# Two MLPs whose first pieces are moved into the stages ahead of them, in a four-layer cross-attention kernel

## The chip, the cores and the metric

The kernel runs on one core of a Trainium2 chip, written directly for the five engines with hand-placed semaphores. TensorE (PE) multiplies and transposes, VectorE (DVE) and ScalarE (ACT) work elementwise, GpSimd (POOL) takes smaller elementwise work, SyncE (SP) issues the DMAs. Each engine runs its own queue strictly in order. The metric is the device time of one launch in microseconds (us), lower is better.

## The reference

Four cross-attention layers run one after the other on x, 8 batches of 256 tokens and 256 features, with a context of 64 tokens a batch. Cut to what matters here:

```python
x = L0(x, ctx, mask)        # 16 heads of 16, residual times tanh(gate)
x = L1(x, ctx, mask)        # 32 query heads, 8 key heads, layer norm behind it
# L2: attention with 16 heads of 16, then an MLP
y = layer_norm(hidden, ln2_w, ln2_b)
x = hidden + gelu(y @ fc_w + fc_b, approximate=True) @ proj_w + proj_b
# L3: two attentions with 16 heads of 128 and a bias key and value, then an MLP
h = layer_norm(x, ln_mlp_scale, ln_mlp_offset)
x = x + gelu(h @ w_fc1 + b_fc1, approximate=False) @ w_fc2 + b_fc2
```

Both MLPs go from 256 to 1024 features and back. "Third layer's MLP" is that of L2, "last MLP" that of L3.

## The kernel before

The work is a chain of stages, each software-pipelined by hand: in every engine's function a Python loop writes the order of its queue, and semaphores (`pe_...`, `a_...`, `d_...`, `p_...` by the engine that counts them up) tie the queues together.

**Small layers.** L0 to L2 are 24 units (layer, batch), u = 0 to 23 (NU = 24), in slots u = 0 to 25. A unit of L2 has two tiles of scores; a unit of L1 has four (NK = 64 tiles in all). For a unit PE makes the source transposes (`source`, L436), values (L481), queries (L518), scores (L546, L552), transposes of the probabilities (L561), transposes of the spread reciprocals (L575, `reciprocals_transposed`, called recT below), the weighted sum (L594) and the output product (L606, L610); a slot mixes pieces of four units. DVE adds the residual (L1118, `unit_residual`), takes maximum and difference of the scores (L1070, L1086), the sums (L1092), and multiplies by the reciprocals (L1105, `unit_normal`). ACT takes the exponentials (L1579) and evicts PSUM (L1586, L1603). In the slots of L2 the MLP's weights are parted into a high part (ACT, L1611, `mlp_weight_high`) and a low part (DVE, L1161, `mlp_weight_low`), one eighth a slot.

**MLPs.** A product is made of three fp32r matmuls, high by high, high by low, low by high (`products`, L631 to L633). A batch b is: source transposes of the normed x (`mlp_source`, L436), scale and offset on DVE (`mlp_affine`, L1020), its high part on ACT (L1623) and low part on DVE (L1175); four groups f of hidden features (`hidden(b, f)`, 12 matmuls each), GELU and high part on ACT (L1722, L1728) and low part on DVE (L1180); then `projected(b)` (48 matmuls) and the residual on DVE (L1270). PE's order before is hidden 0, 1, source of b + 1, projected of b - 1, hidden 2, 3. In batches 2 to 6 DVE also prepares L3's query weights and value sums (L1285, L1293, L1307). The last MLP has the same parts at L1798 and L1426 (weights), L1823, L1469 (source), L1833, L1839, L1475 (hidden).

**L3's attentions** are steps j = -4 to 32 (B = 8, so 4 * B = 32). A step of PE has a key projection (L775), a value projection (L775), scores of tile j (L830, both banks of `scores0` or `scores1`), key products (L847), transposes of tile j - 1 (L862), value products (L880), output of tile j - 1 (L891) and, in even steps, the source of a later batch (L436). Before the softmax's transposes a tile passes maximum (L1378), difference (L1384), exponential (ACT, L1782), sum and reciprocal (L1394 to L1398) and POOL's product with the reciprocals (L2005). The key and value projections end at steps 27 and 29. The last MLP's weights are parted in steps 28 to 31, both parts of two eighths a step; its first source transposes, hidden groups and so on follow only behind step 32, that is behind the last tile's output and residual (L1404).

PSUM has 8 banks: `work0` to `work3`, and `scores0`, `scores1` with two banks each, which are `fbank[0]` to `fbank[3]` for the MLPs. `last_norm` is the layer norm ahead of the last MLP, whose reciprocal root (`rstd`, L1857, L1860) is POOL's.

## Time and profile before

| | |
|---|---|
| median of 3 runs | 1130.79 us (1129.34 to 1131.52) |
| profiled execution | 1130.49 us, span 1128.4 us |
| mean granted PE clock | 0.98 |
| PE busy | 1033.0 us, 92% |
| DVE, ACT, POOL busy | 663.2, 519.1, 402.6 us |

The profile is one execution. A row of the timeline is an instruction or a merged run of them: start, duration, engine, line, operation, output and inputs, count, and in brackets how long the engine stood before it and what ended that wait. A matmul's duration includes its way through the array, so starts, not durations, show the pace. All times are from the span's start.

### The profile page before, as it was taken

How to read it: one execution, taken by the hardware profiler on the slowest of the kernel's cores; microseconds unless marked ns; L12 is line 12 of the kernel's file. 1: busy time of each engine (PE TensorE's matmuls, PEld its weight loads, DVE VectorE, ACT ScalarE, POOL GpSimd, SP SyncE). 2: the span in 40 equal slices, each digit the busy share in tenths (PEclk: the TensorE clock that was granted, in tenths of full speed). 3: DMA queues.
4: the chain of work that ended last, by engine and by line, in shares of the span. 5: the costliest groups of instructions: out<-in, count | busy, mean ns of one | idle time of the engine just before them, and what ended most of it. 6: DMA issues, size and time to landing. Idle time of an engine off the chain costs nothing.

```text
span 1128.4 us, 17672 instructions
## 1 busy us (share of the span) xinstructions
PE 1033.0 (92%) x7036; PEld 810.7 (72%) x7036; DVE 663.2 (59%) x1127; ACT 519.1 (46%) x1036; POOL 402.6 (36%) x416
## 2 busy tenths in 40 slices
PE   6999889887789799989999999999999999978997
PEld 3666555555566699887787777777777777648997
DVE  3657888778568669722444545775444454574552
ACT  2556777676566454433333332333323333324543
POOL 2534578688966523200222112331122211222230
PEclk9999999998999999999999999999999999999999
DMA  9000000000000060010000013310000000100000
GB/s 307 36 2 1 1 1 1 1 1 1 1 1 1 24 220 1 1 53 23 1 1 1 1 49 102 112 38 1 1 1 1 1 1 7 69 1 1 29 19 29
DMA packets 17046, 32.26 MB, mean 29 GB/s; under 512 B 3522, under 2 KB 8388, under 8 KB 16452
## 3 DMA queue, kind: packets, MB, share of 16 engines
q1 hardware_dynamic: 16964, 31.13, 8.1%
q8 instruction: 56, 0.92, 0.3%
q14 instruction: 26, 0.21, 0.1%
HBM read 29.03 MB, written 2.10 MB: 28 GB/s over the span
## 4 chain that ended last, share of the span: by engine, by line
PE 74%; ACT 8%; POOL 7%; issue 5%; DVE 5%; DMA 0%; POOLq 0%; DVEq 0%; ACTq 0%
PE work L775 10%; PE work L891 10%; PE scores L830 9%; PE work L847 5%; PE work L880 4%; PE work L561 3%; PE work L631 3%; PE work L632 3%; PE work L633 3%; PE scores L631 3%; PE scores L633 3%; PE scores L632 2%; PE work L518 2%; PE work L862 2%; PE work L436 2%
## 5 line engine op out<-in xcount | busy, mean ns | idle before, releaser
L891 PE MATMUL work<-pair,probsT 128*128 128x256 f32 x512 | 120.3, 388 | 11.0 <-ACT pair L1777 8.8
L1857 POOL TENSOR_SCALAR stat<-stat 128x2 f32<-128x2 f32 (+1 forms) x49 | 11.1, 227 | 315.4 <-DVE stat L1008 313.9
L891 PEld LDWEIGHTS work<-pair,probsT 128*128 128x128 f32 x512 | 95.7, 192 | 35.3 <-issue 20.3
L775 PE MATMUL work<-ctxT,w 128*128 128x128 f32 x1008 | 118.2, 275 | 2.7 <-ACT pair L1777 1.1
L775 PEld LDWEIGHTS work<-ctxT,w 128*128 128x128 f32 x1008 | 116.3, 192 | 4.1 <-issue 2.0
L830 PE MATMUL scores<-pair,act_bufs 128*128 128x512 f32 x256 | 115.2, 592 | 0.0
L1768 ACT ACTIVATE pair<-work 128x512 f32<-128x512 f32 x64 | 38.2, 598 | 154.5 <-PE work L847 154.5
L1758 ACT ACTIVATE kvT<-work,cols 128x128 f32<-128x128 f32 x124 | 35.5, 369 | 153.2 <-PE work L775 153.2
L2005 POOL TENSOR_TENSOR probs<-probs,smax 128x1024 f32<-128x1024 f32 x22 | 42.0, 1907 | 157.6 <-DVE smax L1398 157.6
L1378 DVE TENSOR_REDUCE smax<-scores 128x16 f32<-128x1024 f32 x32 | 39.2, 1225 | 77.2 <-PE scores L830 77.2
L830 PEld LDWEIGHTS scores<-pair,act_bufs 128*128 128x128 f32 x256 | 46.3, 190 | 46.0 <-issue 45.9
L1369 DVE TENSOR_TENSOR kvT<-work,cols 128x512 f32<-128x512 f32 x32 | 22.1, 691 | 93.1 <-PE work L775 93.1
L847 PEld LDWEIGHTS work<-kvT,w 128*128 128x128 f32 x512 | 61.9, 192 | 15.4 <-issue 15.4
L1070 DVE TENSOR_REDUCE smax<-scores 128x16 f32<-128x1024 f32 x48 | 57.9, 1205 | 20.1 <-PE scores L552 19.4
L847 PE MATMUL work<-kvT,w 128*128 128x128 f32 x512 | 62.4, 275 | 1.8 <-ACT kvT L1758 1.8
L880 PE MATMUL work<-w,kvT 128*64 128x256 f32 x512 | 62.3, 385 | 0.0
L561 PEld LDWEIGHTS work<-ident,pair 128*128 128x128 f32 x256 | 30.0, 150 | 40.6 <-ACT pair L1579 30.6
L561 PE MATMUL work<-ident,pair 128*128 128x128 f32 x256 | 37.7, 294 | 22.1 <-ACT w L1586 13.3
L1586 ACT ACTIVATE w<-work 128x512 f32<-128x512 f32 x88 | 47.6, 593 | 14.4 <-PE work L561 14.3
L1910 POOL TENSOR_TENSOR x<-x,rows_late 128x512 f32<-128x512 f32 x32 | 50.2, 1572 | 9.9 <-DVE act_bufs L1014 8.2
L1014 DVE TENSOR_SCALAR act_bufs<-x,stat 128x256 f32<-128x256 f32 x58 | 44.0, 800 | 14.9 <-POOL stat L1860 14.9
L1898 POOL TENSOR_TENSOR pair<-probs 128x512 f32<-128x512 f32 x32 | 40.9, 1278 | 29.8 <-ACT probs L1579 29.6
(194 smaller groups left out, 2634.0 us busy)
## 6 DMA issues: line engine op xcount, KB each, us to landing
w<-in_l_wk SPq DMA_DIRECT2D x8, 512.0 KB, 6.1
w<-in_l_wq SPq DMA_DIRECT2D x8, 512.0 KB, 6.7
w<-in_l_wo SPq DMA_DIRECT2D x8, 512.0 KB, 7.5
w<-in_l_wv SPq DMA_DIRECT2D x8, 512.0 KB, 5.4
out<-x SPq DMA_DIRECT2D x8, 256.0 KB, 2.2
x<-in_x SPq DMA_DIRECT2D x1, 1536.0 KB, 9.3
pair<-in_l_fc SPq DMA_DIRECT2D x1, 1024.0 KB, 7.1
pair<-in_l_pr SPq DMA_DIRECT2D x1, 1024.0 KB, 9.1
```

Of the source, the lines that this page charges most:

```text
L561: last = tr(work[half][:, q * P:(q + 1) * P], probs[k % 4][:, (4 * half + q) * P:(4 * half + q + 1) * P], ident[:, :])
L631: mm(bank, s_hi, m_hi, start=start, stop=False)
L632: mm(bank, s_hi, m_lo, start=False, stop=False)
L633: return mm(bank, s_lo, m_hi, start=False, stop=stop)
L775: last = mm(bank[:, h * P:(h + 1) * P], w[:, c, (4 * g + h) * K3:(4 * g + h + 1) * K3], ctxT[:, c, p * P:(p + 1) * P], start=(c == 0), sto ...
L830: last = mm(sc[j % 2][:, half * BANK:(half + 1) * BANK], fixed[j // 2 % 2][:, c, t * P:(t + 1) * P], pk[n % 2][:, bb, c, half * BANK:(half ...
L847: last = mm(step_banks(j)[2 + c][:, h * P:(h + 1) * P], w3_wq[:, 4 * g + h, c * P:(c + 1) * P], kvT[i % 2][:, h, :], start=True, stop=True)
L880: last = mm(bank[h * S:(h + 1) * S, bb * D:(bb + 1) * D], kvT[2][:, 2 * q + h, bb * S:(bb + 1) * S], w3_wo[:, 4 * g + 2 * q + h, :], start ...
L891: last = mm(step_banks(j + 1)[0][:, 0:D], probsT_bufs[j % 2][:, q, :], pv[n % 2][:, bb, q, :], start=(q == 0), stop=(q == GH // 2 - 1))
L1070: v.tensor_reduce(smax[k % 2][:, 0:GH], s3, X, ALU.max).then_inc(d_max, 1)
L1586: act(pT[:, 4 * half:4 * half + 4, t, :], work[half][:, :].rearrange("p (q n) -> p q n", n=P), ACT.Copy).then_inc(a_pT, 1)
L1910: g.tensor_tensor(xb(b), xb(b), row(name).unsqueeze(1).broadcast_to([P, TT, D]), ALU.add).then_inc(done, 1)
```

## The change

Nothing of the computation changes; instructions move between queues and within them, with the semaphores that this needs.

- Slots: `mlp_weight_low` goes from near the start of DVE's slot to its end. Stats and norm of the third layer MLP's batch 2 leave slot 23 and follow in the MLP's batch 0, as later batches' do.
- Third layer's MLP: `mlp_source(0)` is in PE's slot 23, in bank `work[3]` instead of `fbank[3]`; in slot 24 `hidden(0, 0)` stands ahead of recT, which now also waits for `mlp_affine`, and `hidden(0, 1)` ahead of the output. PE's order in a batch becomes hidden 0, 1, source, hidden 2, projected, hidden 3, and DVE's and ACT's orders follow.
- The first two key projections of L3 stand ahead of `projected(7)`, in `fbank[0]` and `fbank[1]`; later banks wait for the last residual (`d_mr`).
- Last MLP: `last_norm` in steps 28 and 29 instead of 30 and 31, `last_source(0)` in step 30, `last_affine(0)` and `last_low(0)` on DVE in step 30, ACT's source high part in step 31, `last_hidden(0, 0..3)` and `last_source(1)` in step 32 ahead of the last tile's transposes, ACT's first two GELU groups ahead of its `tile_out(31)`. The weights' low parts go from DVE to POOL (`weight_low`, semaphore `p_wl`).

```diff
         def key_bank(i):
-            return fbank[0] if i == 1 else step_banks(i - 4)[0]
+            return fbank[i] if i < 2 else step_banks(i - 4)[0]
...
+        def mlp_bank(b):
+            return work[3] if b == 0 else work[2 + b % 2]
...
 tensor, reciprocals_transposed(u)
+                if u == NU - 1:
+                    e.wait_ge(d_mT, 2)
...
 tensor, slots
-                    if u == NU:
-                        mlp_source(0)
                     for k in late:
                         probs_transposed(k)
                     if tiles:
                         scores(*tiles_of(u)[1])
+                    if u == NU:
+                        hidden(0, 0)
                     if u > 0:
                         reciprocals_transposed(u - 1)
                         weighted(u - 1)
                     if u == NU:
-                        hidden(0, 0)
+                        hidden(0, 1)
...
+                if u == NU - 1:
+                    mlp_source(0)
                 if u > 0:
                     output(u - 1)
-            for f in range(1, 4):
-                hidden(0, f)
-                if f == 2:
-                    mlp_source(1)
-            for b in range(1, B + 1):
-                for f in range(2):
-                    if b < B:
-                        hidden(b, f)
+            hidden(0, 2)
+            mlp_source(1)
+            hidden(0, 3)
+            for b in range(1, B):
+                hidden(b, 0)
+                hidden(b, 1)
                 if b + 1 < B:
                     mlp_source(b + 1)
+                hidden(b, 2)
                 projected(b - 1)
-                for f in range(2, 4):
-                    if b < B:
-                        hidden(b, f)
+                hidden(b, 3)
...
+            for i in range(2):
+                key_projection(i - 4, i)
+            projected(B - 1)
             for j in STEPS:
...
+                if j == 4 * B:
+                    for f in range(4):
+                        last_hidden(0, f)
+                    last_source(1)
                 if tile_of(j - 1) is not None:
                     tile_transposed(j - 1)
...
+                if j == 4 * B - 2:
+                    last_source(0)
...
 vector, slots
-                for q in mlp_pieces(u - 1):
-                    mlp_weight_low(q)
+                if u == NU:
+                    mlp_affine(0)
                 if u >= 2:
                     unit_residual(u - 2)
+                if u == NU:
+                    mlp_source_low(0)
-                if NU - 3 <= u < NU:
+                if NU - 3 <= u < NU - 1:
                     mlp_stats(u - NU + 3)
...
                 if tiles:
                     tile_sums(tiles[0][0])
+                for q in mlp_pieces(u - 1):
+                    mlp_weight_low(q)
...
 vector, a batch of the third layer's MLP
+                mlp_hidden_low(b, 2)
+                if b + 2 < B:
+                    mlp_stats(b + 2)
+                    mlp_norm(b + 2)
                 if b == 1:
                     ln_row_differences()
...
                 if b > 0:
                     mlp_residual(b - 1)
-                for f in range(2, 4):
-                    if b < B:
-                        mlp_hidden_low(b, f)
-                if b + 3 < B:
-                    mlp_stats(b + 3)
-                    mlp_norm(b + 3)
+                mlp_hidden_low(b, 3)
...
 vector, steps
-                if j >= 4 * B - 4 and j < 4 * B:
-                    for q in range(2):
-                        weight_low((j - 28) // 2, 2 * (j % 2) + q)
-                if j in (4 * B - 2, 4 * B - 1):
-                    last_norm(j - 4 * B + 2)
+                if j in (4 * B - 4, 4 * B - 3):
+                    last_norm(j - 4 * B + 4)
+                if j == 4 * B - 2:
+                    last_affine(0)
+                    last_low(0)
...
 scalar, steps
+                if j == 4 * B - 1:
+                    source_high(0)
+                if j == 4 * B:
+                    last_hidden(0, 0)
+                    last_hidden(0, 1)
                 if tile_of(j - 1) is not None:
                     tile_out(j - 1)
...
 gpsimd
+            def weight_low(w, q):
+                both = w1_parts if w == 0 else w2_parts
+                n = raw.shape[2] // 4
+                e.wait_ge(a_wh, 8 + 4 * w + q + 1)
+                g.tensor_tensor(flat(both[1])[:, q * n:(q + 1) * n], raw[:, w, q * n:(q + 1) * n],
+                                flat(both[0])[:, q * n:(q + 1) * n].bitcast(F32), ALU.subtract).then_inc(p_wl, 1)
...
-                if j in (4 * B - 2, 4 * B - 1):
-                    rstd(("m3", j - 4 * B + 2), TT)
+                if j in (4 * B - 4, 4 * B - 3):
+                    rstd(("m3", j - 4 * B + 4), TT)
+                if 4 * B - 4 <= j < 4 * B:
+                    for q in range(2):
+                        weight_low((j - 28) // 2, 2 * (j % 2) + q)
```

## Rows read from the trace of the kernel before

**Rows 1.** The page's first part: busy us, share of the span, instructions

```profile
PE 1033.0 (92%) x7036; PEld 810.7 (72%) x7036; DVE 663.2 (59%) x1127; ACT 519.1 (46%) x1036; POOL 402.6 (36%) x416
```

**Rows 2.** PE's waits, 303 to 393 us: total, times, longest

```profile
PE work L436 <- DVE x L1118: 7.8, 4, 3.5
PE work L610 <- DVE pair L1105: 1.8, 1, 1.8
PE work L575 <- POOL pair L1888: 1.8, 1, 1.8
PE scores L631 <- issue: 1.5, 1, 1.5
PE work L561 <- ACT pair L1579: 1.1, 1, 1.1
```

**Rows 3.** Windows: length, PE, PEld, DVE, ACT, POOL busy, clock, DMA, GB/s

```profile
355.00:366.00 11.00, 10.93 (x83) 7.70 (x82) 9.45 (x17) 6.57 (x13) 7.14 (x8) 1.00 0.00 0
...
413.98:425.90 11.92, 11.92 (x102) 11.92 (x101) 10.67 (x25) 6.31 (x14) 5.06 (x4) 1.00 0.00 0
...
438.17:453.86 15.69, 13.63 (x103) 13.42 (x102) 14.40 (x31) 6.30 (x14) 5.17 (x4) 0.89 0.01 2
```

**Rows 4.** PE's waits, 960 to 1129 us

```profile
PE work L862 <- POOL probs L2005: 6.1, 1, 6.1
PE scores L631 <- ACT src_high L1823: 3.9, 2, 2.5
```

**Rows 5.** Timeline, ACT and DVE in slots 17, 19 and 23

```profile
305.12 1.09 ACT L1568 ACTIVATE act_bufs<-x,stat 128x256 f32<-128x256 f32 x2 [2.38 <-POOL stat L1866]
...
320.51 1.27 DVE L1161 TENSOR_TENSOR m_w_low<-pair,m_w_high 128x512 fp32r<-128x512 f32 x1 [3.29 <-ACT m_w_high L1611]
...
373.43 1.13 DVE L1014 TENSOR_SCALAR act_bufs<-x,stat 128x256 f32<-128x256 f32 x2
```

**Rows 6.** Timeline, PE in slots 18, 19 and 23

```profile
308.89 1.98 PE L481 MATMUL work<-w,ctxT 128*64 128x256 f32 x8
...
323.02 1.08 PE L481 MATMUL work<-w,ctxT 128*64 128x256 f32 x8
...
377.60 3.42 PE L610 MATMUL work<-w,pair 128*128 128x256 f32 x8 [1.85 <-DVE pair L1105]
```

**Rows 7.** Timeline, PE: first matmul of `hidden(1, 0)`; key product 1

```profile
397.62 0.55 PE L631 MATMUL scores<-m_src_high,m_w_high 128*128 128x256 f32 x1 [2.29 <-ACT m_src_high L1623]
...
509.08 2.02 PE L847 MATMUL work<-kvT,w 128*128 128x128 f32 x16 [1.81 <-ACT kvT L1758]
```

**Rows 8.** Timeline, DVE: two residuals of the third layer's MLP

```profile
438.84 0.68 DVE L1270 TENSOR_TENSOR x<-work,x 128x512 f32<-128x512 f32 x1
...
453.04 0.68 DVE L1270 TENSOR_TENSOR x<-work,x 128x512 f32<-128x512 f32 x1
```

**Rows 9.** Groups by line: busy, mean ns, idle before, releasers

```profile
L1898 POOL TENSOR_TENSOR pair<-probs 128x512 f32<-128x512 f32 x32 | 40.9, 1278 | 29.8 <-ACT probs L1579 29.6
...
L1722 ACT ACTIVATE pair<-scores,cols 128x256 f32<-128x256 f32 x64 | 26.8, 470 | 32.5 <-PE scores L633 32.5
...
L1728 ACT ACTIVATE m_hid_high<-pair 128x512 fp32r<-128x512 f32 x32 | 20.2, 632 | 1.0
```

**Rows 10.** Timeline around the last tiles and in the last MLP

```profile
989.98 1.28 DVE L1426 TENSOR_TENSOR w_low<-w,w_high 128x512 fp32r<-128x512 f32 x2
...
998.21 3.60 PE L830 MATMUL scores<-pair,act_bufs 128*128 128x512 f32 x8
...
998.89 4.01 DVE L1426 TENSOR_TENSOR w_low<-w,w_high 128x512 fp32r<-128x512 f32 x2
...
1005.58 1.22 DVE L1378 TENSOR_REDUCE smax<-scores 128x16 f32<-128x1024 f32 x1
...
1013.24 1.97 PE L862 MATMUL work<-ident,probs 128*128 128x128 f32 x8 [6.10 <-POOL probs L2005]
...
1037.28 2.28 POOL L1910 TENSOR_TENSOR x<-x,rows_late 128x512 f32<-128x512 f32 x1 [0.85 <-DVE act_bufs L1014]
```

More of the change, by code:

```diff
@@ L645, in mlp_source @@
                     e.wait_ge(d_mT, 2 * (b - 2) + 2)
-                transposes(fbank[3] if b == 0 else work[2 + b % 2], norm[(B + b) % 3]).then_inc(pe_mx, 1)
+                transposes(mlp_bank(b), norm[(B + b) % 3]).then_inc(pe_mx, 1)
             def hidden(b, f):
@@ L779, in first_free @@
             def first_free(j):
+                e.wait_ge(d_mr, B)
                 e.wait_ge(a_pk, 2 * keys_before(j))
@@ L790, in third_free @@
             def third_free(j):
+                if j > -4:
+                    e.wait_ge(d_mr, B)
                 e.wait_ge(a_lk, keys_before(j))
@@ L794, in fourth_free @@
             def fourth_free(j):
+                if j > -4:
+                    e.wait_ge(d_mr, B)
                 e.wait_ge(d_vT, values_before(j))
@@ L1169, in mlp_affine @@
                     e.wait_ge(a_sh, b - 2)
-                affine(fbank[3] if b == 0 else work[2 + b % 2], srcT[i % 3], "l2_g2", "l2_b2", d_mT)
+                affine(mlp_bank(b), srcT[i % 3], "l2_g2", "l2_b2", d_mT)
             def mlp_source_low(b):
@@ L1730, in scalar @@
             for b in range(B):
-                mlp_hidden(b, 0)
-                mlp_hidden(b, 1)
-                if 0 < b and b + 1 < B:
-                    mlp_source_high(b + 1)
-                mlp_hidden(b, 2)
-                if b == 0:
-                    mlp_source_high(1)
+                for f in range(3):
+                    mlp_hidden(b, f)
+                    if f == (2 if b == 0 else 1) and b + 1 < B:
+                        mlp_source_high(b + 1)
                 mlp_hidden(b, 3)
@@ L1798, in weight_high @@
                 act(flat(both[0])[:, q * n:(q + 1) * n], raw[:, w, q * n:(q + 1) * n], ACT.Copy).then_inc(a_wh, 1)
-            for j in STEPS:
-                key, value = key_of(j), value_of(j)
-                if key is not None:
-                    key_bias(key)
-                    key_products(key)
-                if tile_of(j - 1) is not None:
-                    tile_out(j - 1)
-                if tile_of(j) is not None:
-                    tile_exponentials(j)
-                if value is not None:
-                    value_products(value)
-                if j >= 4 * B - 4 and j < 4 * B:
-                    for q in range(2):
-                        weight_high((j - 28) // 2, 2 * (j % 2) + q)
             def source_high(b):
@@ L1839, in last_hidden @@
                 act(hid_parts[b % 2][0][:, 2 * f:2 * f + 2, :], hid_whole[f], ACT.Copy).then_inc(a_hh, 1)
-            source_high(0)
-            for b in range(B):
-                for f in range(2):
-                    last_hidden(b, f)
-                if b + 1 < B:
-                    source_high(b + 1)
-                for f in range(2, 4):
-                    last_hidden(b, f)
+            for j in STEPS:
+                key, value = key_of(j), value_of(j)
+                if key is not None:
+                    key_bias(key)
+                    key_products(key)
+                if j == 4 * B - 1:
[3 more added lines that the diff above has]
+                    last_hidden(0, 1)
+                if tile_of(j - 1) is not None:
+                    tile_out(j - 1)
+                if tile_of(j) is not None:
+                    tile_exponentials(j)
+                if value is not None:
+                    value_products(value)
+                if j >= 4 * B - 4 and j < 4 * B:
+                    for q in range(2):
+                        weight_high((j - 28) // 2, 2 * (j % 2) + q)
+            for b in range(B):
+                for f in range(3):
+                    if b > 0 or f == 2:
+                        last_hidden(b, f)
+                    if f == (2 if b == 0 else 1) and b + 1 < B:
+                        source_high(b + 1)
+                last_hidden(b, 3)
         def gpsimd(e):
```

177 lines of the change are left out of this document (82 added, 95 removed).

## The prediction

> **What bounds the kernel now.** I read the page first: TensorE (PE) is busy 92% of the span [rows 1], so what can be won is its idle time, and the lower clock that follows some of it. A list of PE's waits by window says where that is. In the small units' last slots PE waits four times on the residual (L1118), 7.8 us in all with 3.5 the longest, and four more times for 1.8, 1.8, 1.5 and 1.1 us [rows 2]. In the third layer's MLP the pace is 11.92 us a batch, but one batch took 15.69 us with 14.40 us of VectorE (DVE) in it [rows 3]: there DVE is the bound. At the end PE waits 6.1 us for the last tile's probabilities and 3.9 us in two waits on the MLP's source [rows 4]. Elsewhere PE runs without a gap. So I place the moved instructions in each engine's in-order queue and follow the chain in these four places.
>
> **Part 1, low parts of the MLP weights moved in DVE's queue (slots 18 to 21).** DVE stood 3.29 us before L1161, waiting for ScalarE's (ACT's) high part, and the residual that PE's next source transposes need was queued behind it [rows 5]. Now `mlp_weight_low` is last in the slot, and its high part is a slot old. The residual then starts when PE's output ends. In three slots the wait of (7.8 - 3.5) / 3 = 1.4 us goes, 4.3 us together, if nothing else takes the place. The slot ahead of the last two, whose PE queue has no source, shows what is then the bound: 11.00 us with PE busy 10.93 and DVE 9.45 [rows 3]. So it should hold. In slot 18 the next thing late is ACT's norm of the source, which begins at 305.12 and takes 1.09 [rows 5], so the source can start at 306.3 instead of 308.3: 2.0 us. The eight matmuls behind that 3.5 us wait took 1.98 us against 1.08 in the next slot [rows 6], the granted clock at its lower level, 1.2 GHz; in proportion for the eight transposes behind them this is 1.5 us more, which I count as saved because an idle of half the length was not followed by it in slots 19 to 21. Part 1: 4.3 + 2.0 + 1.5 = 7.8 us; bounds 4.3 (slot 18 gives nothing) and 8.2.
>
> **Part 2, third layer's MLP begun in the last two slots.** From the end of `weighted(22)` to the end of `output(23)`, which ACT's first GELU waits for by the code, PE idles 6.2 us in four waits [rows 2], and the eight matmuls of `output(22)` took 3.42 us at the lower clock [rows 6], of which I count 1.5 us as lost to it. The stats and norm of batch 2 leave slot 23 (the norm alone took 1.13 us [rows 5], the stats as an estimate 0.9), so `unit_normal(22)`, which `output(22)` waits for, comes 1.7 us sooner; the source transposes of batch 0 (0.4 us) fill part of what is left. `recT(23)` now also waits for DVE's `mlp_affine(0)`, since the source sits in `work[3]`; affine runs right after slot 23's last instructions, and `hidden(0, 0)` waits for ACT's high and DVE's low part of it. Following the queues I find idles of 0.4, 0.5 and 0.7 us left, 1.6 in all. `hidden(0, 1)` (12 matmuls, 1.4 us) is now ahead of `output(23)`. So: 6.2 + 1.5 - 1.6 - 1.4 = 4.7 us. From there ACT's chain (table load, three GELU groups, source high part) is unchanged, so `hidden(1, 0)` stays as far behind `output(23)` as it was [rows 7]; PE only idles longer in front of it, with the same stretch at the lower clock. Bounds 2.5 (slot 23 has the same waits) and 6.2.
>
> **Part 3, order within the MLP and two key projections.** From `hidden(1, 0)` at 397.62 [rows 7] to `key_products` of key 1 at 509.08 [rows 7] are 111.5 us. PE's own work is 720 matmuls at 0.120 us (11.92 less 0.36 for four transposes, over 96 [rows 3]), six sources at 0.36, and two key projections and one key product, each 16 matmuls like those of [rows 7] at some 1.85 us: 86.7 + 2.2 + 5.5 = 94.4. Now DVE, the bound in batches 2 to 5: residual to residual it needs 14.2 us (438.84 to 453.04 [rows 8]) for PE's 11.92. The new order gives it the same instructions, but hidden's third low part is now ahead of the long sums, and it waits for ACT: after the source's high part ACT needs two GELUs and a high part, 2 x 0.47 + 0.63 = 1.6 us [rows 9], while DVE has one low part of 0.7 us to do [rows 10]. That makes 15.0 a batch. PE has one more hidden group (1.4 us) of lead before `projected(b - 1)`, so I find PE idle 0.3, 3.2, 1.8 and 3.1 us in batches 3 to 6, 8.4 in all, and three stretches at the lower clock of 1.7 us (PE busy 13.63 against 11.92 us for one matmul more [rows 3]), the first behind `hidden(1, 0)`. At the end the wait for the last low part is gone, since the key projections cover it; the 1.8 us that key product 1 waits for ACT's `key_bias` [rows 7] stays, because ACT's order of keys is unchanged. 94.4 + 8.4 + 5.1 + 1.8 = 109.7, against 111.5; the walk through the queues, stretch by stretch, gives 108.4. I take 3 us saved. Bounds: 0 (every batch DVE-bound until the end) and 5.5 (low part 2 does not wait). SyncE's four value-weight loads still start at the end of `projected(7)`; what covers them is now two key products and a key projection instead of these and one projection more, and if that were short the first value projection would stand for the difference. Key and query weights are loaded long before. The added waits on `d_mr` B are satisfied by the last residual, right after `projected(7)` and while PE has a key product of 2 us, so nothing queued behind them waits.
>
> **Part 4, last MLP ahead of the last tile's end.** DVE loses eight low parts and PE gets `last_source(0)` in step 30 and four hidden groups plus `last_source(1)` in step 32, 6.2 us of work, ahead of `tile_transposed(31)`. Before, two low parts took DVE from 998.89 to 1002.9 and two norms followed, so the last tile's maximum began at 1005.58 although its scores were done at 1001.8 (998.21 and 3.60) [rows 10]. Now `last_affine(0)` and `last_low(0)` stand there instead, behind ACT's source high part, and they too hold the last maximum, to 1004.6 at best and 1006.7 if the norms of steps 28 and 29 are late. The last transposes can thus start at 1012.3 to 1014.5 instead of 1013.24; but PE no longer waits for them. Removed are 6.1 + 3.9 us of idle [rows 4], and 2.3 us of lower clock go (the transposes took 1.97 us [rows 10], twice their 1.0, and the output behind them in the same way). New is this: `tile_residual(31)` stands in DVE's queue ahead of `last_affine(1)`, so source 1 starts only when PE's last output has ended; residual, low, affine, high, low take 3.7 us, in which PE has nothing, and 1.7 us of lower clock follow. New too are about 2 us of waits in steps 29 to 31. 10.0 + 2.3 - 3.7 - 1.7 - 2 = 4.9, say 5.0. Bounds 1 and 6.7. After that batches run at PE's pace as before, and the end is the same, since the last group still waits for the whole chain.
>
> What the eight low parts cost on GpSimd (POOL): 1.28 us each by the nearest two-input form on POOL [rows 9], 10 us over four steps, on an engine that is busy 36% of the span [rows 1]; upper bound 2.28 each, what POOL's row addition took beside DVE [rows 10]. They matter by what they hold up on DVE. Two DVE low parts took 4.01 us beside POOL and 1.28 us without it [rows 10]: one engine stood while the other ran. The Trainium skill's page SBUF — State Buffer, section "Who interferes with whom", states that a DVE instruction with two SBUF inputs and a GpSimd instruction that reads SBUF exclude each other, whoever issues first; the trace agrees. By it the norms of steps 28 and 29, which follow POOL's rstd, would stand behind low parts; that is the first rival below, with 1115 us where my sum has 1110.
>
> **The sum.** Against the profiled execution's 1130.5 us (span 1128.4, 2.1 around it; 0.3 under the median of the runs): 7.8 + 4.7 + 3.0 + 5.0 = 20.5 us, so 1110.0 us.
>
> **Rivals.**
> - *POOL's low parts hold DVE up.* If each norm of steps 28 and 29 waits for two of them (2.6 us) and `last_low(0)` for one more (1.3), scores 30 and 31 and the last maximum are 6.5 us late and part 4 gives nothing: 1115. For: the 4.01 us. Against: DVE no longer has the low parts, 4.01 us in one step, to do itself.
> - *The DVE-bound MLP gives nothing back and slot 23 stays as it is.* Part 3 at 0, part 2 at 2.5: 1130.5 - 7.8 - 2.5 - 5.0 = 1115. For: DVE 14.40 of 15.69 us. Together with the first: 1120.
> - *All covers hold.* Parts at 8.2, 5.5, 5.5 and 6.7: 1104.6.
> - *Slower.* All eight POOL low parts lie on the last softmax chain at 2.28 us, 18.2 us, with nothing gained in part 4: 1130.5 - 15.5 + 18.2 = 1133. It decides only from a loss of 15.5 us in steps 28 to 32. Against: POOL's idle time [rows 1].
> - *No effect.* Each removed wait is replaced by the next one behind it (ACT's norm in the slots, DVE in the MLP, affine at the end): 1130.
>
> **Chances and range.** Forecast (1107 to 1113) 0.52; POOL rival 0.14; DVE rival 0.14; both 0.05; all covers 0.09; no effect 0.03; slower 0.03. 0.94 lie at faster; "within 0.2%" is 2.3 us, about what a measurement of this kernel can tell from no change. The range 1103 to 1119 takes in the forecast, the covers and each of the two rivals alone.
>
> **What would show it.** Part 1: source transposes of slots 19 to 21 without idle. Part 2: `hidden(1, 0)` starts 12.5 us sooner, at 385.1. Part 3: PE's waits on the hidden parts total some 8 us, the last `projected` has none, DVE's residuals 15.0 us apart. Part 4: no idle before the last transposes, one of 3 to 4 us before `hidden(1, 0)`. It would be wrong if the slots were held by POOL's sums instead, or if steps 28 to 31 grew by more than 2 us.

## The result and the profile after

The changed kernel takes 1113.34 us (median of 4 runs, 1112.15 to 1115.3) against 1131.15 us beside it: ratio 0.9847, 95% interval 0.9828 to 0.9867. The prediction was 1110.0 us in a range of 1103 to 1119. The profiled execution took 1112.15 us, span 1110.1.

The page's line of busy times, as in [rows 1]: PE idles 15 us less than before (span less busy time: 80.8 for 95.4 us), DVE has 6 us of work less, ACT the same, POOL 5 us more.

```profile
PE 1029.3 (93%) x7036; PEld 808.8 (73%) x7036; DVE 657.2 (59%) x1119; ACT 519.7 (47%) x1036; POOL 407.5 (37%) x424
```

PE's waits from 303 to 385 us, which answer to [rows 2] (total, times, longest). The residual (now L1135) is in none of them.

```profile
PE work L440 <- ACT act_bufs L1579: 1.6, 1, 1.6
PE scores L637 <- issue: 1.1, 1, 1.1
PE work L616 <- DVE pair L1122: 0.4, 1, 0.4
PE work L565 <- ACT pair L1590: 0.2, 1, 0.2
```

The same from 385 to 500 us, the third layer's MLP. The four waits "<- issue" of L637 stand before `projected`, which by the code waits for the last low part of hidden; the profile itself names no releaser there.

```profile
PE work L637 <- issue: 9.9, 4, 3.8
PE scores L637 <- ACT m_src_high L1634: 3.7, 1, 3.7
PE work L856 <- issue: 1.8, 1, 1.8
PE work L780 <- ACT pair L1776: 0.8, 1, 0.8
```

And from 960 us to the end, which answers to [rows 4]. The 6.1 us for the last probabilities are gone; of the source's waits one is left, of 3.5 us. The 2.4 us are before the last `projected`; the kernel before has them as well.

```profile
PE scores L637 <- ACT src_high L1815: 3.5, 1, 3.5
PE work L637 <- ACT hid_high L1831: 2.4, 1, 2.4
PE work L903 <- ACT pair L1785: 2.3, 1, 2.3
PE work L903 <- ACT probsT L1797: 2.2, 3, 0.7
PE work L874 <- DVE kvT L1384: 0.7, 1, 0.7
```

Three rows of PE's timeline cut the span into stretches: `hidden(1, 0)` of the third layer's MLP, key product 1 (both answer to [rows 7]) and `hidden(1, 0)` of the last MLP.

```profile
385.82 0.55 PE L637 MATMUL scores<-m_src_high,m_w_high 128*128 128x256 f32 x1 [3.74 <-ACT m_src_high L1634]
...
497.15 2.02 PE L856 MATMUL work<-kvT,w 128*128 128x128 f32 x16 [1.76 <-issue]
...
1013.47 0.40 PE L637 MATMUL scores<-src_high,w_high 128*128 128x256 f32 x1 [3.46 <-ACT src_high L1815]
```

In the kernel before they stand at 397.62, 509.08 and 1031.76 us. So the first stretch gave 11.8 us, the second 0.1 (111.46 to 111.33), the third 6.4 (522.68 to 516.32), and the tail behind them nothing. That is the 18.3 us between the two profiled executions. The second stretch, for which the prediction had 3 us, is the one to explain. Here it is as one window, first of the kernel before, then of the changed one (length; busy time of PE, PEld, DVE, ACT, POOL; clock; DMA):

```profile
397.62:509.08 111.46, 101.61 (x792) 100.26 (x793) 71.62 (x146) 47.58 (x101) 23.80 (x21) 0.94 0.19 68
...
385.82:497.15 111.33, 99.66 (x793) 98.80 (x793) 76.81 (x152) 47.28 (x101) 28.20 (x24) 0.96 0.15 55
```

So the same length hides two changes: PE waits 11.7 us in it instead of 9.7, and it is busy 2.0 us less for the same work, at a mean granted clock of 0.96 instead of 0.94.

### The profile page after: what moved, and what is told of

The parts are those of the page before. It is cut to its first block, busy times and chain, and to the rows that moved or that the text cites. A ratio compares the mean times of both kernels' runs of the same rounds, so it can differ in the third digit from the quotient of the medians.

```text
span 1110.1 us, 17681 instructions
## 1 busy us (share of the span) xinstructions
PE 1029.3 (93%) x7036; PEld 808.8 (73%) x7036; DVE 657.2 (59%) x1119; ACT 519.7 (47%) x1036; POOL 407.5 (37%) x424
## 4 chain that ended last, share of the span: by engine, by line
PE 77%; ACT 7%; POOL 7%; issue 5%; DVE 3%; DMA 0%; POOLq 0%; DVEq 0%; ACTq 0%
PE work L903 10%; PE work L780 10%; PE scores L839 10%; PE work L856 5%; PE work L892 4%; PE work L565 3%; PE work L637 3%; PE scores L637 3%; PE work L639 3%; PE work L638 3%; PE scores L638 3%; PE scores L639 3%; PE work L522 3%; PE work L616 2%; PE work L440 2%
## 5 line engine op out<-in xcount | busy, mean ns | idle before, releaser
L1031 DVE TENSOR_SCALAR act_bufs<-x,stat 128x256 f32<-128x256 f32 x58 | 46.4, 843 | 16.4 <-POOL stat L1872 16.4
L1910 POOL TENSOR_TENSOR pair<-pair 128x512 f32<-128x512 f32 x32 | 41.7, 1303 | 26.0 <-ACT pair L1590 25.5
```

The source lines that it names most:

```text
L1910: g.tensor_tensor(halves, e3[:, :, 0:n], e3[:, :, n:S], ALU.add).then_inc(p_half, 1)
```

## Where the second stretch's gain went

Windows from residual to residual of the third layer's MLP (length; busy time of PE, PEld, DVE, ACT, POOL; clock; DMA). Before the change such a batch was 14.2 us long [rows 8]; now it is 16.0, with DVE busy for 14 of them:

```profile
431.94:447.96 16.02, 13.66 (x100) 13.49 (x100) 13.97 (x28) 6.26 (x13) 5.72 (x4) 0.89 0.01 2
447.96:463.97 16.01, 13.63 (x100) 13.45 (x100) 13.96 (x29) 6.25 (x13) 5.71 (x4) 0.89 0.00 1
```

DVE's timeline in the first of them:

```profile
436.82 0.69 DVE L1197 TENSOR_TENSOR m_hid_low<-pair,m_hid_high 128x512 fp32r<-128x512 f32 x1 [0.70 <-ACT m_hid_high L1739]
...
439.54 0.74 DVE L1031 TENSOR_SCALAR pair<-x,stat 128x256 f32<-128x256 f32 x2 [1.15 <-POOL stat L1872]
...
441.32 1.51 DVE L1302 CUSTOM_DVE_ANT_0 pair<-w,pair,cols 128x256 f32<-128x256 f32 x1
...
442.77 0.48 DVE L1302 CUSTOM_DVE_ANT_0 pair<-w,pair,cols 128x256 f32<-128x256 f32 x1
...
443.99 4.06 DVE L1324 SCALAR_TENSOR_TENSOR pair<-w,cols,pair 128x256 f32<-128x256 f32 x4
```

And POOL's beside it, its row addition and the scaling of the query weights:

```profile
440.36 2.20 POOL L1922 TENSOR_TENSOR x<-x,rows_late 128x512 f32<-128x512 f32 x1 [0.85 <-DVE pair L1031]
...
444.15 2.58 POOL L1998 TENSOR_TENSOR w<-w,pair 128x1024 f32<-128x1024 f32 x1 [1.59 <-DVE pair L1302]
```

Of the 1.8 us more, 0.70 are the predicted wait for ACT's high part. Another 1.03 are the first of four equal weighted sums (L1302), which takes 1.51 us where the other three take 0.48: it ends 0.3 us after POOL's addition does. In the order of before, the addition (443.56 to 445.22 us in that trace) lay mainly beside the scale and offset (L1020), which read PSUM. The four weighted additions (L1324) look innocent, since they took 4.06 us before as well; runs 3 and 6 show that they are not. The two rows of the kernel before:

```profile
443.56 1.66 POOL L1910 TENSOR_TENSOR x<-x,rows_late 128x512 f32<-128x512 f32 x1 [0.85 <-DVE pair L1014]
...
449.06 4.06 DVE L1307 SCALAR_TENSOR_TENSOR pair<-w,cols,pair 128x256 f32<-128x256 f32 x4
```

## The experiments

Each was timed in five rounds beside the kernel before. B is the stretch from `hidden(1, 0)` to key product 1, C from there to the last MLP's `hidden(1, 0)`, both of the profiled execution. Executions of one kernel scatter by up to 4.5 us (the kernel before by up to 7.7), so the stretches of the trace help with small differences, but they scatter too. C is 516.2 to 516.4 us in seven of the eight executions that have the changed kernel's code there, and 514.65 in the eighth, run 1. B is 111.2 to 111.3 in the changed kernel and in runs 4 and 5, and 114.16 in run 11, though none of these edits the code of B: there PE waits 12.4 us for 11.7, and is busy 2.1 us longer at a mean granted clock of 0.93. A difference of under 3 us in B or under 2 in C is taken as shown below only where rows of the timeline carry it.

| run | edit | median us | ratio, interval | B | C |
|---|---|---|---|---|---|
| - | before | 1131.15 | | 111.46 | 522.68 |
| - | changed | 1113.34 | 0.9847, 0.9828 to 0.9867 | 111.33 | 516.32 |
| 1 | row addition behind scaling | 1115.13 | 0.9856, 0.9825 to 0.9887 | 110.90 | 514.65 |
| 2 | stats in the gap | 1108.28 | 0.9789, 0.9761 to 0.9817 | 105.88 | 516.33 |
| 3 | old order in the batches | 1113.41 | 0.9840, 0.9811 to 0.9869 | 112.96 | 516.24 |
| 4 | last tile's residual later | 1107.99 | 0.9797, 0.9769 to 0.9825 | 111.18 | 512.53 |
| 5 | low parts back on DVE | 1119.37 | 0.9882, 0.9861 to 0.9903 | 111.28 | 521.86 |
| 6 | run 2, scaling on DVE | 1103.76 | 0.9748, 0.9725 to 0.9770 | 101.91 | 516.35 |
| 7 | run 6, rows on DVE | 1102.03 | 0.9733, 0.9711 to 0.9755 | 101.07 | 516.35 |
| 8 | key projections behind | 1118.32 | 0.9874, 0.9853 to 0.9895 | 118.21 | 516.34 |
| 9 | before, part 1 alone | 1119.57 | 0.9893, 0.9871 to 0.9914 | 111.52 | 522.72 |
| 10 | source of batch 1 early | 1112.85 | 0.9834, 0.9809 to 0.9858 | 114.20 | 516.35 |
| 11 | norms ahead of low parts | 1110.26 | 0.9812, 0.9787 to 0.9836 | 114.16 | 513.46 |
| 12 | together | 1091.07 | 0.9643, 0.9630 to 0.9657 | 97.8 | 511.2 |

Run 11's B, beside those of the kernel before and the changed kernel above:

```profile
384.95:499.11 114.16, 101.72 (x793) 100.86 (x793) 76.94 (x152) 47.32 (x101) 28.16 (x24) 0.93 0.14 54
```

**Run 1.** POOL's order in a batch:

```diff
                 rstd(("m2", b), TT)
-                mlp_bias(b)
                 if b >= 4:
                     wq_scaled(1, b - 4)
+                mlp_bias(b)
```

> The changed kernel with one line moved on GpSimd: the row addition of a batch of the third layer's MLP stands behind the scaling of the query weights instead of ahead of it. Theory A (the two engines exclude each other): in the changed kernel the first weighted sum of a batch takes 1.51 us instead of 0.48 because GpSimd's row addition has begun about 1 us before it; without that addition beside it it takes 0.48 again, the residuals stand 15.0 us apart instead of 16.0 in four batches, PE's waits before projected shrink by as much, and the time is 1113.3 - 4 = 1109.5 us. Theory B (the batches are held by something else, PE's order or ScalarE): the sum gets shorter, the distance stays 16.0, 1113. Theory C (the addition only collides elsewhere): 0.5 us or more comes back on the residual or the low parts, 1111 to 1112.

DVE's timeline. The weighted sums are 0.48 us each again, and the four behind them take 5.00 us instead of 4.06:

```profile
440.92 0.48 DVE L1302 CUSTOM_DVE_ANT_0 pair<-w,pair,cols 128x256 f32<-128x256 f32 x1
...
442.54 5.00 DVE L1324 SCALAR_TENSOR_TENSOR pair<-w,cols,pair 128x256 f32<-128x256 f32 x4
```

The residuals are 15.9 us apart. Theory C: the addition does cost DVE 1.03 us, and moved it costs 0.94 elsewhere. The median is inside the scatter of the changed kernel; the profiled execution (1110.89 us) was the fastest of the five, the others took 1115.05 to 1115.43.

**Run 2.** DVE's order in a batch:

```diff
+                if b + 2 < B:
+                    mlp_stats(b + 2)
                 if b + 1 < B:
                     mlp_source_low(b + 1)
                 mlp_hidden_low(b, 2)
                 if b + 2 < B:
-                    mlp_stats(b + 2)
                     mlp_norm(b + 2)
```

> The changed kernel with one move on VectorE: the stats of batch b + 2 stand ahead of the source's low part of b + 1, their norm behind hidden's third low part. Theory A (VectorE's own queue sets the batch): the 0.70 us wait for ScalarE's high part and the 1.15 us wait for GpSimd's reciprocal root both go, since each now has other work under it; residuals 14.2 us apart instead of 16.0, in four or five batches, 1113.3 - 7 = 1106.5 us; if only one of the waits goes, 15.0 and 1109.5. Theory B (PE's order sets it): 1113. Theory C: the row addition moves with the norm and now meets another instruction; then the 1.03 us of the weighted sum turn up in other rows and the distance is 14.2 all the same.

The wait for ACT is gone, that for POOL's reciprocal root is 0.61 instead of 1.15 us; residuals 14.6 us apart, B 5.4 us shorter. Theory A, with a part of the second wait left: POOL's two instructions of the root, overlapped now by low parts, took 0.58 and 1.12 us instead of 0.22 and 0.72.

**Run 3.** The old order inside the batches, covers kept:

```diff
                     mlp_source(b + 1)
-                hidden(b, 2)
                 projected(b - 1)
+                hidden(b, 2)
                 hidden(b, 3)
...
                     mlp_residual(b - 1)
+                mlp_hidden_low(b, 2)
                 mlp_hidden_low(b, 3)
+                if b + 2 < B:
+                    mlp_stats(b + 2)
+                    mlp_norm(b + 2)
```

> The changed kernel with the old order inside batches 1 to 7 of the third layer's MLP: projected of b - 1 ahead of hidden's third group on PE, and on VectorE the third low part behind the residual and the stats and norm at the end of the batch. The key projections stay ahead of the last projected. Theory A (the new order costs VectorE what it wins PE): residuals 14.2 us apart as before the change instead of 16.0; from hidden(1, 0) to key product 1 111.5 less the 1.3 to 2 us that the key projections cover, so 109.5 to 110 against 111.3, and 1111.5 to 1112 us. Theory B (the new order on PE is worth its lead of a hidden group all the same): the waits before projected grow, 1114 to 1116. Theory C: stats one batch later than before the change come too late for the source transposes, which then wait 1 us or more a batch: 1116 or more.

Theory C's waits came: those before `projected` are gone, and five of 11.3 us in all before the source transposes, for DVE's norm, stand in their place. Its 1116 us did not: the median is that of the changed kernel, and B's 1.6 us more are in these waits but under what B moves by itself. So going back to the old order gains nothing. The batches of this trace show something else, here one of them, on DVE:

```profile
437.67 2.71 DVE L1192 TENSOR_TENSOR m_src_low<-pair,m_src_high 128x512 fp32r<-128x512 f32 x1
...
443.06 2.04 DVE L1324 SCALAR_TENSOR_TENSOR pair<-w,cols,pair 128x256 f32<-128x256 f32 x4
```

and on POOL:

```profile
436.93 2.89 POOL L1998 TENSOR_TENSOR w<-w,pair 128x1024 f32<-128x1024 f32 x1
```

POOL's scaling here meets the source's low part, which takes 2.71 us instead of 0.69, and the four L1324 take 2.04 us, half of the 4.06 that they took in both kernels beside the scaling. That points to 2.0 us of DVE standing behind POOL in every such batch of both kernels; run 6 tries it.

**Run 4.** In the last MLP, `tile_residual(31)` on DVE from ahead of batch 0 to behind `last_low(1)`:

```diff
                 if b + 1 < B:
                     last_low(b + 1)
+                if b == 0:
+                    tile_residual(4 * B - 1)
                 hidden_low(b, 2)
```

> The changed kernel with the last tile's residual moved on VectorE behind the second source's low part of the last MLP. Theory A (the residual in the queue is the whole of PE's 3.46 us wait before hidden(1, 0)): affine can run at 1004.7, the high part by 1008.2, the low part by 1008.9, before the last output ends at 1010; no wait, and no stretch at the lower clock of 1.5 us behind it: 1113.3 - 5.0 = 1108.3 us. Theory B (the stretch at the lower clock comes anyway, from the short waits around the last output): 1110. Theory C (ScalarE's order, source behind the third GELU group, is late as well): a wait of 1 us or more stays, 1111.

`hidden(1, 0)` follows the last output at 1008.97 us with no wait and at full clock; C gained 3.8, and behind it PE waits 1.0 us for the norm of batch 2, the next thing late. Theory A.

**Run 5.** The last MLP's eight low parts on DVE again, ahead of the norms of steps 28 and 29:

```diff
 vector, steps
+                if 4 * B - 4 <= j < 4 * B:
+                    for q in range(2):
+                        weight_low((j - 28) // 2, 2 * (j % 2) + q)
                 if j in (4 * B - 4, 4 * B - 3):
                     last_norm(j - 4 * B + 4)
```

> The changed kernel with the last MLP's eight weight low parts back on VectorE, in steps 28 to 31, ahead of the norms there. Theory A (two-input work on GpSimd and on VectorE excludes each other): the norms of these steps take 0.74 us again instead of 2.62, which gives VectorE 1.9 us in each of two steps, and the low parts cost it 1.28 us a step plus their wait for ScalarE's high parts, which the maximum of the next tile then stands behind. From key product 1 to the last hidden(1, 0) this is between 514.5 and 518 us where the changed kernel has 516.3; I take 517 and 1114. Theory B (moving them to GpSimd was most of this part's gain, since VectorE has no room): tiles 29 to 31 are each 1.3 us late and more, 1118. Theory C (they lie beside PE's work on either engine): 516.3 and 1113.3.

C is 5.5 us longer: theory B, and the estimate of 517 missed. The norms take 0.74 us again, but the low parts stand in the tiles' chain, and not for 1.28 us a step but for 2.38, 1.28, 4.00 and 3.47. The third pair, on DVE,

```profile
992.10 4.00 DVE L1441 TENSOR_TENSOR w_low<-w,w_high 128x512 fp32r<-128x512 f32 x2
```

meets POOL's product and addition, as in [rows 10]:

```profile
991.98 1.90 POOL L2033 TENSOR_TENSOR probs<-probs,smax 128x1024 f32<-128x1024 f32 x1 [6.38 <-DVE smax L1413]
993.84 1.71 POOL L1932 TENSOR_TENSOR x<-x,rows_late 128x512 f32<-128x512 f32 x1
```

Behind it stands DVE's scale and offset for the last MLP, and for that PE waits 2.57 us at 997.16, a wait that the changed kernel doesn't have; the output after it took 6.56 us where it took 3.72, at the lower clock. That is most of the 5.5 us.

```profile
997.16 1.17 PE L874 MATMUL work<-ident,probs 128*128 128x128 f32 x8 [2.57 <-DVE act_bufs L1037]
```

**Run 6.** Run 2, and the scaling on DVE:

```diff
             def wq_biased(a, g):
...
+                if a == 1:
+                    e.wait_ge(d_wt, 4 * n + 4)
+                    v.tensor_tensor(w, w, ln_rows[:, 0, a - 1, :].unsqueeze(1).broadcast_to([P, 4, D]),
+                                    ALU.mult).then_inc(p_wg, 1)
...
 gpsimd
-                if b >= 4:
-                    wq_scaled(1, b - 4)
```

> The kernel of the second run with one more move: the scaling of the first attention's query weights by a row (128x1024, 2.58 us on GpSimd) is done on VectorE, just ahead of the addition of the bias to them. Theory A (exclusion): the four scalar_tensor_tensor of a batch, 4.06 us in all with it beside them, take 2.04, so VectorE loses 2.0 us of standing and gains one instruction of 1.22 us: residuals 13.8 us apart instead of 14.6 in four batches, 1108.3 - 3.2 = 1105 us, although VectorE is given more work. Theory B (engine load): VectorE, the bound, gets 1.22 us more a batch, 15.8 us apart, 1108.3 + 4.9 = 1113.

DVE's timeline:

```profile
434.99 2.20 DVE L1314 TENSOR_TENSOR w<-w,pair 128x1024 f32<-128x1024 f32 x1
...
438.74 2.04 DVE L1328 SCALAR_TENSOR_TENSOR pair<-w,cols,pair 128x256 f32<-128x256 f32 x4
440.69 0.68 DVE L1287 TENSOR_TENSOR x<-work,x 128x512 f32<-128x512 f32 x1
```

The engine that sets the batch has one instruction of 1.22 us more (L1314; 2.20 here, since the row addition holds it up now) and is 0.8 us a batch faster: residuals 13.8 us apart, B 4.0 us shorter. This decides for theory A against engine load. It doesn't hang on the scatter of B: the distance of the residuals, 16.0 us in the changed kernel, is within 0.1 us of that in runs 4, 5, 8, 10 and 11, which leave these batches alone.

**Run 7.** The row additions of batches 4 to 7 on DVE too, behind the norm:

```diff
+                if 4 <= b + 2 < 8:
+                    e.wait_ge(*NORMS["m2", b + 2])
+                    e.wait_ge(s_in["rows_late"], 16)
+                    v.tensor_tensor(xb(b + 2), xb(b + 2), row("l2_pb").unsqueeze(1).broadcast_to([P, TT, D]),
+                                    ALU.add).then_inc(p_xm, 1)
```

> The kernel of the run before with the row additions of batches 4 to 7 of the third layer's MLP on VectorE as well (0.7 us each by the other 128x512 additions; 1.7 to 2.2 us on GpSimd). Theory A: the 1.03 us by which the addition held a weighted sum up go and 0.7 us come: residuals 13.4 to 13.5 us apart, another 1.3 us in all, 1103.5. Theory B (engine load): 0.7 us more a batch, 3 us slower than the run before. Theory C: from 13.8 us on PE, with 12.3 us of its own a batch, or ScalarE's chain is the bound, and nothing changes.

13.54 us apart, B 0.8 us shorter: theory A's sign and distance. The medians, 1.7 us apart, have overlapping intervals.

**Run 8.** The changed kernel with the key projections behind `projected(7)`:

```diff
+            projected(B - 1)
             for i in range(2):
                 key_projection(i - 4, i)
-            projected(B - 1)
```

> The changed kernel with the first two key projections of the fourth layer behind the third layer's last projected again, as in the kernel before, but in the same banks as now. Theory A (they cover the last low part): PE waits 1.3 to 2.4 us before the last projected, which the changed kernel doesn't, and the time is 1113.3 + 1.8 = 1115. Theory B (what they cover comes back behind them, since key product 1 waits for ScalarE's key bias, which runs while projected goes on in the changed kernel): the wait of 1.8 us before key product 1 is still there, and the total 1117. Theory C (the cover is worth nothing, the wait only moves): 1113.3.

B is 6.9 us longer than in the changed kernel, but not all of it is the edit's:

```profile
384.47:502.68 118.21, 103.43 (x793) 102.39 (x793) 76.92 (x152) 47.26 (x101) 28.15 (x24) 0.92 0.17 60
```

2.4 us are a new wait before the last `projected`. From 485 to 495 us, behind it, the mean granted clock is 0.83 of full where the changed kernel has 1.00, which is 1.7 us more. The rest, 2.8 us, is lower clock behind `hidden(1, 0)` (0.72 for 0.83 from 385 to 395 us) and at 465 to 475 us (0.83 for 1.00), and run 11, which doesn't touch this code, has it in both places too. Against run 11 the edit costs 4.0 us in B; by the medians it costs 5.0. The wait before key product 1 is still 1.76. Nearest to theory B.

**Run 9.** The kernel before with `mlp_weight_low` at the end of DVE's slot, nothing else (part 1 of the prediction alone).

> The kernel before with one edit alone: VectorE's low parts of the third layer's MLP weights at the end of a slot instead of near its start. Theory A (part 1 stands for itself, 7.8 us by the prediction, 8.1 in the trace of the changed kernel): the scores of slot 22 begin 7 us sooner than in the kernel before, and the time is 1130.5 - 8 = 1122.5 us. Theory B (slots 22 to 24 take it back, since there the low parts now stand ahead of nothing and the residual's wait was the cover for others): 1126. Theory C (it takes more than its own, as the later low parts no longer hold anything in slots 22 to 24 up either): 1121.

`hidden(1, 0)` starts at 388.08 us instead of 397.62, that is 9.5 us sooner, B and C as before the change. Theory C: of the 12.9 us that parts 1 and 2 gave, this edit alone gives 10: 8.1 up to slot 22 and 2.0 in slots 22 to 24. Of these 2.0 us 1.4 are clock: `output(22)` waits the same 1.85 us as in [rows 6], but its matmuls take 1.99 us instead of 3.42. Whether that is the edit's or the execution's isn't shown.

```profile
369.47 1.99 PE L610 MATMUL work<-w,pair 128*128 128x256 f32 x8 [1.85 <-DVE pair L1105]
```

PE's waits from 303 to 388 us, to set beside [rows 2]: the four for the residual are gone, one of 1.6 for ACT's norm stands for the first of them, and slots 23 and 24 keep theirs, most of which part 2 then removed.

```profile
PE work L610 <- DVE pair L1105: 1.9, 1, 1.9
PE work L575 <- POOL pair L1888: 1.8, 1, 1.8
PE work L436 <- ACT act_bufs L1568: 1.6, 1, 1.6
PE scores L631 <- issue: 1.5, 1, 1.5
```

**Run 10.** ACT's `mlp_source_high(1)` behind the first GELU group, DVE's affine and low part likewise:

```diff
-                    if f == (2 if b == 0 else 1) and b + 1 < B:
+                    if f == (0 if b == 0 else 1) and b + 1 < B:
                         mlp_source_high(b + 1)
```

> The changed kernel with the source of batch 1 of the third layer's MLP earlier: ScalarE's high part stands behind the first GELU group instead of the third, VectorE's affine ahead of the first low part and its low part behind it. Theory A (the 3.7 us before hidden(1, 0) are ScalarE's queue): the high part comes at 381.7 instead of 384.4, hidden(1, 0) starts at 383.0 instead of 385.8, and all that follows with it: 1113.3 - 2.8 = 1110.5 us, 1.5 less if the stretch at the lower clock behind the wait goes as well. Theory B (VectorE sets the batches behind it): hidden(1, 0) is 2.8 us sooner, but the residuals of batches 2 and on stand where they stood, 1113.

`hidden(1, 0)` starts at 382.47, 3.4 us sooner than in the changed kernel, and all but 0.5 us of it is lost by key product 1: B is 2.9 us longer, 2.7 of them waits of PE. The first thing in the way is a new wait of PE for the norm of batch 2, which the change had taken out of slot 23:

```profile
388.06 1.12 PE L440 MATMUL work<-ident,act_bufs 128*128 128x128 f32 x4 [2.49 <-DVE act_bufs L1031]
```

**Run 11.** POOL in steps 28 and 29:

```diff
+                    if j < 4 * B - 2:
+                        e.wait_ge(*NORMS["m3", j - 4 * B + 4])
                     for q in range(2):
                         weight_low((j - 28) // 2, 2 * (j % 2) + q)
```

> The changed kernel with one wait more on GpSimd: in steps 28 and 29 the two weight low parts wait for VectorE's norm of that step. Theory A (the norms stood for 1.9 us behind the low parts): they take 0.74 us instead of 2.62, the value bias comes 1.9 us sooner, and the 0.7 us wait of PE's transposes in step 28 goes; of the second norm's 1.9 us the maximum of tile 30 gets 1.3 at most and PE, which is behind, nothing: 1113.3 - 1 = 1112.3 us. Theory B (what the norms gain, the value bias and the maxima behind them lose, since the low parts now stand there): no difference, or 0.5 us slower. Theory C (the low parts come too late for the last MLP's hidden groups, which start at 998): slower by 1 us or more.

The norms take 0.74 us instead of 2.62 and 2.63, and the 0.7 us wait in step 28 is gone. C is 2.9 us shorter, but 1.7 of them are clock. Every execution had the same 2.3 us wait before the output of tile 28; in the changed kernel's the output ran at the lower clock,

```profile
974.88 5.38 PE L903 MATMUL work<-pair,probsT 128*128 128x256 f32 x16 [2.31 <-ACT pair L1785]
```

in run 1's, with nothing changed near it, at the full one, as in run 11's:

```profile
974.28 3.69 PE L903 MATMUL work<-pair,probsT 128*128 128x256 f32 x16 [2.31 <-ACT pair L1785]
```

Against run 1 the edit is worth 1.2 us, which is theory A. It may be worth more: of the ten executions with the 0.7 us wait in step 28, 4 us ahead, all but run 1's ran that output at the lower clock (5.30 to 5.38 us); of the four without it (before, runs 9, 11 and 12) only run 12's did. So the edit gives 1.2 to 2.9 us, and which isn't settled. The medians are 3.1 us apart.

**Run 12.** Runs 7, 4, 10 and 11 in one kernel, with two edits aimed at waits that these had shown. On DVE the stats of batch 2 stand first in the MLP and their norm behind `mlp_source_low(1)`; on ACT:

```diff
                 if key is not None:
-                    key_bias(key)
+                    if key != 1:
+                        key_bias(key)
+                    if key == 0:
+                        key_bias(1)
                     key_products(key)
```

> The kernel of the seventh run (1102.0 us) with the edits of the fourth, tenth and eleventh and what was late behind two of them: in the last MLP the last tile's residual stands behind the third batch's norm as well; GpSimd's low parts of steps 28 and 29 wait for the norms; the source of batch 1 of the third layer's MLP is early, and now the stats and norm of batch 2 stand ahead of and behind it, so that PE's next source transposes don't wait 2.5 us for them; ScalarE makes the key bias of key 1 ahead of the key products of key 0, so that key product 1 doesn't wait 1.8 us. Theory A (each wait of PE is its own): 5.3 for the fourth run's edit and 1.0 for the norm ahead of it, 2.9 for the eleventh's, 3 for the source, 1.8 for the key: 1102.0 - 14 = 1088 us, and 1086 with the stretches at the lower clock. Theory B (the third layer's MLP is bound by VectorE in batches 2 to 5 still, 13.5 us for PE's 12.3, and takes the source's 3 us back): 1091. Theory C (waits move on): 1094 or more.

1091.07 us, 3.6% under the kernel before and 22 us under the changed one. PE's waits in the MLP, from 375 to 505 us:

```profile
PE work L637 <- issue: 2.8, 2, 1.4
PE scores L637 <- ACT m_src_high L1652: 1.3, 1, 1.3
PE work L780 <- ACT pair L1794: 0.8, 1, 0.8
```

B is 97.8 us, where PE's own work is 94.4. The time is theory B's 1091, but by another way. B's reason was that DVE's batches take the source's 3 us back. In batches 3 to 5 the residuals are still 13.54 us apart, yet they come 4.0 us sooner than in run 7, and key product 1 comes 5.9 us sooner, where theory A had 4.8 for the two edits of this MLP. C is what fell short: 5.1 us shorter than run 7's, with the tail behind it no shorter, where 9.2 were expected of the edits of the last steps. 1.7 of the rest are the output of tile 28, which ran at the lower clock again (5.38 us). No run takes the others apart.

## Why the prediction was right, and where it was not

The time lay 3.3 us from the forecast and inside the range, in part by luck: the stretches gave 8.1, 4.8, 0.1 and 6.4 us for 7.8, 4.7, 3.0 and 5.0, so part 3 fell short by 2.9 us, and part 4 gave 1.4 of that back. The 1.2 us by which slot 18 began later belong to the execution and come off the total.

- **Part 1** (7.8 us) measured 8.1: scores of slot 22 at 350.54 instead of 357.50, from a point in slot 18 that lay 1.2 us later although nothing had moved ahead of it. Slots 19 to 21 have no wait at the source, slot 18 one of 1.56 for ACT's norm, as written. What the prediction did not see is that the same edit can also give 2 us in slots 22 to 24 (run 9), among them the 1.5 us of lower clock that it had put down to part 2.
- **Part 2** (4.7) measured 4.8: waits of 0.4, 0.2 and 1.1 us where it had 0.4, 0.5 and 0.7. `hidden(1, 0)` started at 385.82, forecast 385.1. Part 2 was never run by itself.
- **Part 3** (3.0) measured 0.1. The mechanism was right, DVE-bound batches and a covered end, and the sizes were off. The step that failed is "that makes 15.0 a batch": it was 16.0. The step before it is where it went wrong: "the new order gives it the same instructions", priced as before. One took 1.03 us more, because POOL's row addition now fell beside it. By the prediction's own sum, PE's waits before `projected` were 9.9 us and not 8.4; with its 94.4 of PE work, the 1.8 before key product 1 and 5.2 us of lower clock (99.66 us busy less the 94.4; 5.1 predicted) that gives 111.3. The other 1.2 us was the choice of 3 between the sum's 1.8 and a walk's 3.1. That it netted nothing hides two large terms: the key projections' cover is worth 4 to 5 us (run 8), and DVE's longer batches ate it (14.2 to 16.0 us, three times).
- **Part 4** (5.0) measured 6.4. No wait before the last transposes, 3.46 us before `hidden(1, 0)` (3.7 predicted), 1.5 us of lower clock behind it (1.7). Against it stand 1.7 us of lower clock at the output of tile 28, which the kernel before ran in 3.69 us; without them part 4 is 8.1. The "2 us of waits in steps 29 to 31" were the 0.7 in step 28 and little else. Run 4 shows that the 3.46 us are `tile_residual(31)` in DVE's queue alone.
- **The first rival** (POOL's low parts hold DVE up) was true as a mechanism, 1.9 us on each of two norms, and small as a price: 1.2 us of PE's time, at most 2.9 (run 11). On DVE the same low parts would have cost 5.5 us (run 5). Where it decided was not in this part but in part 3.
- **The DVE rival** held for the batches, part 3 at 0.1 where it had 0, and not for slot 23.

The Trainium skill's page SBUF — State Buffer, section "Who interferes with whom", has the rule that fits the two-input instructions of runs 1, 3, 5 and 6: of a DVE instruction with two SBUF inputs and a GpSimd instruction that reads SBUF, whichever comes second waits for the whole of the first. The traces agree in both directions: a DVE sum of 0.48 us took 1.51, and GpSimd's root of 0.72 us took 1.12. The norms, which the prediction also put under this rule, have one SBUF input; the same section counts `tensor_scalar` from SBUF to SBUF among the instructions that can contend through their 2-port modes, and here they did, 2.62 us for 0.74. The prediction weighed this rule for part 4 and did not ask it of part 3, where POOL's instructions had not been edited at all.

## What to carry to other kernels

When an order is changed on one engine, the others' instructions slide along it: for an engine that bounds a stretch, look at what each of its two-input instructions will lie beside on POOL, and take its duration alone from where nothing does. A duration that is the same in both kernels can still hold a wait, as the 4.06 us of L1324 did; moving POOL's work onto the bound engine can then make that engine faster, as in run 6. Each wait taken away shows the next (the norm behind the residual, the norm of batch 2 behind the source), so count a gain only up to the next thing late. And compare a stretch first with an execution that doesn't edit it: B moved by 2.8 us with no edit in it.

## What the runs showed that was not expected

- Four DVE instructions of 0.48 us took 4.06 us together beside one POOL instruction of 2.58, and 2.04 without it: DVE stood for most of POOL's instruction.
- A clamp of 128x16 that takes 0.17 us took 1.22 beside POOL's low part in the last tile of the changed kernel, and the norm, a one-input instruction from SBUF to SBUF, 2.62 instead of 0.74.
- After one and the same wait of 2.3 us PE's next 16 matmuls took 5.38 us in some executions and 3.69 in others: the granted clock alone moves an execution of these matmuls by 1.7 us. Over the whole of B, with no edit in it, run 11 was 2.8 us longer than the changed kernel.
